# A new order of scores, values and outputs at the 64 attention slices of a gated cross-attention and feed-forward block

## Chip, cores and metric

One Trainium2 chip, one core. The metric is the device time of one execution in microseconds (us). Engines: PE is TensorE (matmuls; PEld its weight loads), DVE is VectorE, ACT is ScalarE, POOL is GpSimd, SP the queue that issues the DMAs.

## The reference, cut to what matters

```python
# x, ctx: (32, 64, 512); 8 key heads, 4 query heads for each, head size 128; causal inside each 64 rows
x = x + tanh(g_xattn) * attention(layernorm(x), ctx, ctx, Wq, Wk, Wv) @ Wd.T
x = x + tanh(g_ffn) * ffn(layernorm(x))
# attention: scores = Q K^T / sqrt(128), masked, softmax over the keys, times V
# ffn: down(silu(gate(x)) * up(x)), each weight being w * (su @ sv), inner size 1792
```

All is float32. Every large product is made as three products of fp32r numbers (high*high, high*low, low*high), so each operand is first split into `hi` (ACT copies it to fp32r) and `lo` (DVE or POOL subtracts).

## The kernel before

The 2048 rows are 16 tiles of 128. The program is written engine by engine, in an order set by hand, with semaphores between the engines; nothing reorders it. Stages: keys of half the chunks, then 56 "quads" `quad(q)` (values, keys, queries; also the effective ffn weights through `effective`), then 64 units of attention, then 28 steps of the ffn. A unit `u` is one key head and one chunk of 256 rows, two units are a pair, `NU = 64`, `NPAIR = 32`. The last three quads already hold the first units: `scores(0)`, `scores(1)` stand before quad 53 (`NQ - 3`), `scores(2)`, `scores(3)` before quad 55, `weighted_values(0)` inside it.

What one unit takes, with the lines of the profile:
- `scores(u)`, L697: 8 matmuls of K (128 rows, 64 columns of weights) by Q into one PSUM bank, `score_bank(u)`, 6 for even and 7 for odd units.
- `turned` (DVE transpose out of the bank, L1334), `masked` (POOL, L1657), `maxima` (DVE, L1338), `other_maxima` (four small ACT copies, L1022), `row_maxima` (DVE, L1344), `less_max` (POOL, L1663), `exponentials` (ACT, L1035), `sums` (DVE, L1348), `other_sums` (four ACT copies, L1030), `inverse` (DVE, L1352 and L1356), `over_sum` (POOL, L1669), `probs_turned` (DVE, L1362). Maxima and sums are shared by the two units of a pair.
- `weighted_values(u)`, L722: 8 matmuls with 64-row weights, into two banks; `out_hi` (ACT, two halves, L1042) and `out_lo` (DVE, two halves, L1375) split the result.
- `output(i)`, `i = 2u` and `2u + 1`: 12 matmuls of 512 columns (L574) into one bank; `add_to_x(i)` (DVE, L1386) adds it to the rows `X`. `output_hi`, `output_lo` (ACT L1015, POOL L1649) split the four heads of the next output weights; each takes 1 of 4 `e`.

PE's loop body of pair p (u = 2p), before: scores(u), scores(u+1), output(2u-7), output(2u-6), weighted_values(u-2), weighted_values(u-1), output(2u-5), output(2u-4).

In pairs 18, 21, 24, 27 (`ROWS1`) the second layernorm of two finished tiles is started: `stats2`, `ln_moments` (DVE, L1239 to L1250), `ln_pow` (POOL, L1600), `apply2` (POOL, L1677, two passes). One pair later (`COLUMNS1`) `columns2` transposes them on PE (L751) into banks 2 and 3 between output(2u-7) and output(2u-6), `x2_columns` (ACT, L1050, L1053) empties these banks, and `x2_sums` (POOL) combines; weighted_values(u-1), which writes the same banks, waits for `x2_columns`. Another pair later (`SPLIT1`) come `x2_hi_of` (ACT, L1068) and `x2_lo_of` (DVE, L1410).

Two waits matter later and are the same in both kernels: `out_hi(u-1)` overwrites what output(2u-5) reads, and so waits for that output's end; `out_lo` of it follows.

Of the kernel before, what the change touches and what calls it, by code (L numbers as in the profile page):

```python
# [21 lines left out]
NU = HKV * NCH  # L22
# [29 lines left out]
def flamingo(nc, es, x, ctx_t, g_xattn, g_ffn, w1, wq, wd, wf, sf_l, sf_r, out):  # L52
# [150 lines left out]
    a_c0, a_chi, a_k, a_w1, a_tanh = sem("a_c0"), sem("a_chi"), sem("a_k"), sem("a_w1"), sem("a_tanh")  # L203
    a_xt, a_xhi, a_wa, a_s1, a_s5, a_c11 = (sem("a_xt"), sem("a_xhi"), sem("a_wa"), sem("a_s1"), sem("a_s5"),
# [87 lines left out]
    def output_bank(i):  # L292
        if i >= 2 * NU - 4:
            return 4 + i - (2 * NU - 4)
        return 6 if i % 4 == 3 else (3 * (i // 4) + i % 4) % 2

    def output_before(i):

        n = 3 * (i // 4) + i % 4 - 2
        return 4 * (n // 3) + n % 3  # L300

    def score_bank(u):
        return 6 + u % 2
# [34 lines left out]
    def _(sp):  # L338
# [148 lines left out]
        for q in range(NQ):  # L487
            quad_dmas(q)
            if q == NQ - 3:
                load_wd(1)  # L490
            if q == NQ - 2:
                load_q_k(2)
                load_q_k(3)
            if q == NQ - 1:
# [5 lines left out]
                load_v(3)  # L500
            if q == Q0 + NHP:
# [67 lines left out]
    def _(pe):  # L569
# [42 lines left out]
        def effective(m):  # L612
# [4 lines left out]
            if m == E_AT[NQ - 3]:  # L617
                pe.wait_ge(v_turn, 2)
            if m == E_AT[NQ - 1]:
                pe.wait_ge(v_turn, 4)  # L620
# [63 lines left out]
        def scores(u):  # L684
# [41 lines left out]
        def output(i):  # L726
# [20 lines left out]
        def columns2(m, banks):  # L747
            for p in range(2):
                pe.wait_ge(g_xn, 2 * m + p + 1)
# [14 lines left out]
        output(0)  # L764
        for p in range(2, NPAIR):
            u = 2 * p
            scores(u)
            scores(u + 1)
            output(2 * u - 7)
# [5 lines left out]
            weighted_values(u - 1)  # L775
# [1081 lines left out]
```

## Time and profile before

| | us |
|---|---|
| median of 3 runs (1431.50, 1431.82, 1435.93) | 1431.82 |
| the profiled execution | 1430.72 |
| its span | 1428.7 |
| outside the span | 2.0 |
| PE busy / DVE busy / POOL busy / ACT busy | 1400.6 / 1016.2 / 1038.6 / 640.3 |

A profile row gives start and duration, the engine, the source line and the operation, and in square brackets the idle time of the engine just before it with what ended it. Matmuls overlap in a pipeline: a row of one is longer than the distance to the next. The granted TensorE clock is 1.00 in all stretches but a few us.

### The profile page before, as it was taken

To read this page: it belongs to the slowest core of one execution; us is meant where nothing else is said; L and a number is where in the kernel's file an instruction comes from. 1 tells how busy PE (TensorE), PEld (TensorE's weight loads), DVE (VectorE), ACT (ScalarE), POOL (GpSimd) and SP (SyncE) were. 2 spreads that over 40 slices of the span, in tenths; PEclk is the share of its full clock that TensorE was granted. 3 is DMA by queue.
4 is the path that set the end of the run, shared out by engine and by line. 5 is a ranking of instruction groups with operands and counts; after the bars stand their busy time and mean duration, and the time that the engine had idled before them with its cause. 6 is when DMAs were issued, how large, how long until landed. Compare 5 with 4: busy or idle time off the path is not lost.

```text
span 1428.7 us, 19944 instructions
## 1 busy us (share of the span) xinstructions
PE 1400.6 (98%) x6810; PEld 1125.3 (79%) x6810; DVE 1016.2 (71%) x1549; ACT 640.3 (45%) x1246; POOL 1038.6 (73%) x919
## 2 busy tenths in 40 slices
PE   8999999999999999999999999999999999999998
PEld 8988788888887767777776766767888888888887
DVE  6487777777465677777776776775688878676776
ACT  6465555554444344443443444444344434343433
POOL 5599999998879556656656777775678886666664
PEclk9999999999999999999999999999999999999999
DMA  8477787778887745434443433331112112212112
GB/s 282 150 251 226 233 270 257 253 254 282 307 264 264 254 156 199 140 125 142 135 152 118 155 116 120 127 132 31 45 45 60 52 45 65 105 47 65 45 59 74
DMA packets 116067, 217.96 MB, mean 153 GB/s; under 512 B 9472, under 2 KB 47616, under 8 KB 113920
## 3 DMA queue, kind: packets, MB, share of 16 engines
q1 hardware_dynamic: 115968, 216.70, 46.1%
q8 instruction: 55, 0.90, 0.3%
q14 instruction: 44, 0.36, 0.1%
HBM read 151.13 MB, written 65.54 MB: 152 GB/s over the span
## 4 chain that ended last, share of the span: by engine, by line
PE 82%; POOL 8%; DVE 4%; issue 3%; ACT 1%; DMA 1%; SPq 0%; DVEq 0%; POOLq 0%; ACTq 0%
PE bank L574 65%; PE bank L848 3%; PE bank L849 3%; PE bank L850 3%; PE bank L697 3%; PE bank L722 3%; POOL prob L1663 2%; POOL xn L1677 1%; POOL wd_lo L1649 1%; POOL prob L1657 1%; POOL prob L1669 1%; DVE X L1386 1%; POOL wa_lo L1643 1%; PE bank L621 1%; DMA q_sb<-q_scratch 0%
## 5 line engine op out<-in xcount | busy, mean ns | idle before, releaser
L574 PE MATMUL bank<-xc,wa_hi 128*128 128x512 f32 x896 | 277.4, 391 | 0.0
L574 PE MATMUL bank<-wd_hi,o_hi 128*128 128x512 f32 x512 | 207.9, 406 | 5.0 <-issue 3.5
L574 PE MATMUL bank<-wd_lo,o_hi 128*128 128x512 f32 x512 | 200.8, 392 | 0.0
L574 PE MATMUL bank<-wd_hi,o_lo 128*128 128x512 f32 x512 | 199.5, 390 | 0.0
L574 PEld LDWEIGHTS bank<-xc,wa_hi 128*128 128x128 f32 x896 | 167.7, 188 | 36.4 <-issue 1.1
L574 PE MATMUL bank<-xc,wa_lo 128*128 128x512 f32 x448 | 174.5, 390 | 0.0
L1455 DVE SCALAR_TENSOR_TENSOR X<-bank,tg,X 128x512 f32<-128x512 f32 x221 | 154.5, 742 | 0.0
L574 PE MATMUL bank<-x_hi,wf_hi 128*128 128x512 f32 x392 | 153.0, 390 | 0.0
L574 PE MATMUL bank<-x_hi,wf_lo 128*128 128x512 f32 x392 | 152.6, 389 | 0.0
L574 PE MATMUL bank<-x_lo,wf_hi 128*128 128x512 f32 x364 | 141.7, 389 | 0.0
L1669 POOL TENSOR_TENSOR prob<-prob,row_inv 128x512 f32<-128x512 f32 x64 | 72.5, 1153 | 94.6 <-DVE row_inv L1356 94.6
L1386 DVE SCALAR_TENSOR_TENSOR X<-bank,tg,X 128x512 f32<-128x512 f32 x128 | 94.7, 741 | 65.2 <-PE bank L574 65.2
L574 PEld LDWEIGHTS bank<-wd_hi,o_hi 128*128 128x128 f32 x512 | 96.1, 188 | 47.9 <-issue 27.7
L574 PEld LDWEIGHTS bank<-wd_hi,o_lo 128*128 128x128 f32 x512 | 96.3, 188 | 21.3
L574 PEld LDWEIGHTS bank<-wd_lo,o_hi 128*128 128x128 f32 x512 | 96.3, 188 | 17.7
L1022 ACT ACTIVATE other_max<-own_max 32x32 f32<-32x32 f32 x128 | 29.1, 227 | 178.8 <-DVE own_max L1338 176.4
L1657 POOL TENSOR_TENSOR prob<-prob,mask 128x512 f32<-128x512 f32 x64 | 81.2, 1290 | 34.5 <-DVE prob L1334 34.5
L1300 DVE TENSOR_TENSOR t<-bank,s 128x512 f32<-128x512 f32 x44 | 30.3, 689 | 99.9 <-PE bank L574 99.7
L1375 DVE TENSOR_TENSOR o_lo<-bank,o_hi 128x512 fp32r<-128x512 f32 x128 | 82.1, 684 | 23.4 <-ACT o_hi L1042 23.4
L574 PEld LDWEIGHTS bank<-xc,wa_lo 128*128 128x128 f32 x448 | 84.1, 188 | 17.9
L1643 POOL TENSOR_TENSOR wa_lo<-w_raw,wa_hi 128x512 fp32r<-128x512 f32 x72 | 76.5, 1084 | 24.8 <-ACT wa_hi L951 24.7
L1643 POOL TENSOR_TENSOR wa_lo<-ws,wa_hi 128x1024 fp32r<-128x1024 f32 x36 | 92.5, 2570 | 0.0
(181 smaller groups left out, 3424.7 us busy)
## 6 DMA issues: line engine op xcount, KB each, us to landing
q_scratch<-q_st SPq DMA_DIRECT2D x32, 1024.0 KB, 4.4
q_sb<-q_scratch SPq DMA_DIRECT2D x64, 512.0 KB, 4.9
w_raw<-in_wq SPq DMA_DIRECT2D x32, 512.0 KB, 4.4
wd_raw<-in_wd SPq DMA_DIRECT2D x16, 1024.0 KB, 5.1
f_raw<-ffn_eff_scratch SPq DMA_DIRECT2D x28, 512.0 KB, 3.6
er_raw<-in_sf_r SPq DMA_DIRECT2D x42, 256.0 KB, 3.9
e_raw<-in_wf SPq DMA_DIRECT2D x42, 256.0 KB, 5.4
ffn_eff_scratch<-e_eff SPq DMA_DIRECT2D x42, 256.0 KB, 5.2
```

The lines of the kernel that those rows point to most:

```text
L574: last = pe.matmul(to, a, b, start=(start and n == 0), stop=(stop and n == 3 * len(pairs) - 1), skip_group_check=onto)
L697: last = pe.matmul(bank[score_bank(u)][b * S:(b + 1) * S, t * 256:(t + 1) * 256], k_sb[u % 2][:, cb * S:(cb + 1) * S], q_sb[u % 2][:, :, c ...
L722: last = pe.matmul(bank[value_bank(u) + b][:, t * 256:(t + 1) * 256], v_sb[u % 2][rows, t, :], pt_of(u)[rows, t, :], start=True, stop=True)
L848: pe.matmul(to, d_hi[b][:, half, cols], dn_hi[n == NF - 1][:, :], start=True, stop=False)
L849: pe.matmul(to, d_hi[b][:, half, cols], dn_lo[n == NF - 1][:, :], start=False, stop=False)
L850: pe.matmul(to, d_lo[b][:, half, cols], dn_hi[n == NF - 1][:, :], start=False, stop=True).then_inc(p_yf, 1)
L1375: v.tensor_tensor(lo, bank[value_bank(u) + b][:, :].rearrange("p (t e s) -> p t e s", t=CT, e=G), f32(hi), ALU.subtract).then_inc(v_o, 1)
L1386: v.scalar_tensor_tensor(to, bank[output_bank(i)][:, :], tg[:, 0:1], to, ALU.mult, ALU.add).then_inc(v_y, 1)
L1455: v.scalar_tensor_tensor(to, bank[down_bank(n, k)][:, :], tg[:, 1:2], to, ALU.mult, ALU.add).then_inc(v_yf, 1)
L1643: g.tensor_tensor(wa_lo[p][:, part, :, :].rearrange("p n k d -> p (n k d)"), raw, f32(wa_hi[p][:, part, :, :]).rearrange("p n k d -> p (n ...
L1657: g.tensor_tensor(to, to, mask[:, :].rearrange("p (o k) -> p o k", o=1).broadcast_to([P, NR // 2, S]), ALU.add).then_inc(g_mask, 1)
L1669: g.tensor_tensor(to, to, row_inv[:, u % 2, :].rearrange("p (n o) -> p n o", o=1).broadcast_to([P, NR, HS]), ALU.mult).then_inc(g_p, 1)
```

## The change

The entry and the loop over the pairs get a new order on all engines. On PE the loop body becomes output(2u-7), output(2u-6), weighted_values(u-2), weighted_values(u-1), scores(u+2), scores(u+3), output(2u-5), output(2u-4): the scores stand directly behind the values and are made one pair earlier. Score banks change: units 1 and 3 use bank 5; in the loop, bank 6 is shared with the outputs i % 4 == 1 (before: 3). The engines' lists are moved to suit; `apply2` goes from POOL to ACT, with a shift made on POOL; of each four output-weight heads three are split in even pairs and one in odd pairs; loads of queries and keys are issued earlier.

```diff
@@ banks
-        return 6 if i % 4 == 3 else (3 * (i // 4) + i % 4) % 2
+        return 6 if i > 1 and i % 4 == 1 or i == 2 * NU - 5 else (3 * (i // 4) + SHARED[i % 4]) % 2 if i > 1 else i
+    SHARED = (0, None, 1, 2)
     def score_bank(u):
-        return 6 + u % 2
+        return 5 if u in (1, 3) else 6 + u % 2
     def value_bank(u):
-        return 6 if u == NU - 1 else 2 if u % 2 else 4
-    WD_STEP = {2 * k + 2 + n: (k + 1, (2 * n, 2 * n + 1)) for k in range(NWD - 1) for n in range(2)}
+        return 6 if u in (1, NU - 1) else 2 if u % 2 else 4
+    WD_STEP = {2 * k + 2 + n: (k + 1, ((0, 1, 2), (3,))[n]) for k in range(NWD - 1) for n in range(2)}
@@ SP
         for q in range(NQ):
+            if q == NQ - 2:
+                load_q_k(2)
+                load_q_k(3)
             quad_dmas(q)
...
-            if q == NQ - 2:
-                load_q_k(2)
-                load_q_k(3)
...
+                load_q_k(6)
+                load_q_k(7)
...
-            for n in range(u + 2, min(u + 4, NU)):
-                load_q_k(n)
             load_v(u)
             load_v(u + 1)
+            for n in range(u + 4, min(u + 6, NU)):
+                load_q_k(n)
@@ PE, effective: two waits on v_turn removed; scores
-            if u in (1, 3, 5):
-                pe.wait_ge(v_e, E_AT[(NQ - 4, NQ - 2, NQ - 1)[u // 2]] + 1)
-            if u >= 6 and u % 2 == 0:
-                pe.wait_ge(v_y, 2 * u - 8)
+            if u >= 8 and u % 2 == 0:
+                pe.wait_ge(v_y, 2 * u - 10)
+            if u == 1:
+                pe.wait_ge(a_xt, 16)
+            if u in (4, 5):
+                pe.wait_ge(v_o, 4)
@@ PE, weighted_values
             if u == 0:
-                pe.wait_ge(a_xt, 16)
+                pe.wait_ge(v_turn, 4)
             elif u == 1:
+                pe.wait_ge(v_turn, 3)
+                pe.wait_ge(v_e, NP)
+            elif u == 3:
                 pe.wait_ge(v_c12, NQ)
                 pe.wait_ge(v_c21, NQ)
@@ PE, output
-            elif i < 2 * NU - 4 and i % 4 == 3:
-                pe.wait_ge(v_turn, min(2 * ((i + 5) // 4), NU - 2) + 1)
+            elif i == 2 * NU - 5:
+                pe.wait_ge(v_y, i - 1)
+            elif i == 2:
+                pe.wait_ge(v_y, 2)
+            elif i < 2 * NU - 4 and i % 4 == 1:
+                pe.wait_ge(v_turn, min((i + 7) // 2, NU - 2) + 1)
@@ PE, the loop
         weighted_values(1)
         output(0)
+        output(1)
+        scores(4)
+        scores(5)
         for p in range(2, NPAIR):
             u = 2 * p
-            scores(u)
-            scores(u + 1)
-            output(2 * u - 7)
+            if p > 2:
+                output(2 * u - 7)
             if p in COLUMNS1:
                 pe.wait_ge(v_o, 2 * u - 4)
                 columns2(COLUMNS1[p], (2, 3))
             output(2 * u - 6)
             weighted_values(u - 2)
             weighted_values(u - 1)
+            if p + 1 < NPAIR:
+                scores(u + 2)
+                scores(u + 3)
             output(2 * u - 5)
             output(2 * u - 4)
@@ ACT
+            if q == NQ - 1:
+                other_maxima(1)
...
+        def apply2(m):
+            a.wait_ge(g_nm, 8 + m + 1)
+            if m:
+                a.wait_ge(p_xt2, 2 * m)
+            for p in range(2):
+                a.activation(xn2[:, p, :], X[:, 2 * m + p, :], ACT.Identity, bias=shift[:, p:p + 1],
+                             scale=rstd[:, p:p + 1]).then_inc(a_xn2, 1)
...
         for p in range(2, NPAIR):
             u = 2 * p
+            exponentials(u)
+            exponentials(u + 1)
+            other_sums(p)
             if p in WD_STEP:
                 k, heads = WD_STEP[p]
                 for e in heads:
                     output_hi(k, e)
             if p in COLUMNS1:
                 x2_columns(COLUMNS1[p], (2, 3))
-            other_maxima(p)
             out_hi(u - 2)
-            exponentials(u)
-            exponentials(u + 1)
+            out_hi(u - 1)
+            if p in ROWS1:
+                apply2(ROWS1[p])
             if p in SPLIT1:
                 x2_hi_of(SPLIT1[p])
-            other_sums(p)
+            if p + 1 < NPAIR:
+                other_maxima(p + 1)
...
-            out_hi(u - 1)
@@ DVE, the last quad: maxima(2), maxima(3), row_maxima(1), out_lo(0) moved in; then
+        out_lo(1)
         sums(2)
         sums(3)
+        add_to_x(0)
         inverse(1)
+        turned(4)
+        turned(5)
+        probs_turned(2)
+        probs_turned(3)
+        add_to_x(1)
+        maxima(4)
+        maxima(5)
+        row_maxima(2)
         for p in range(2, NPAIR):
             u = 2 * p
+            if p > 2:
+                add_to_x(2 * u - 8)
             sums(u)
             sums(u + 1)
+            if p > 2:
+                add_to_x(2 * u - 7)
             inverse(p)
             if p in ROWS1:
                 stats2(ROWS1[p])
                 ln_moments(8 + ROWS1[p])
+            add_to_x(2 * u - 6)
+            out_lo(u - 2)
+            if p + 1 < NPAIR:
+                turned(u + 2)
+                turned(u + 3)
+            probs_turned(u)
+            probs_turned(u + 1)
+            out_lo(u - 1)
+            add_to_x(2 * u - 5)
+            if p in SPLIT1:
+                x2_lo_of(SPLIT1[p])
+            if p + 1 < NPAIR:
+                maxima(u + 2)
+                maxima(u + 3)
+                row_maxima(p + 1)
@@ POOL
         for p in range(2, NPAIR):
             u = 2 * p
-            over_sum(u - 2)
-            over_sum(u - 1)
-            masked(u)
-            masked(u + 1)
+            over_sum(u)
+            over_sum(u + 1)
             if p in COLUMNS1:
                 x2_sums(COLUMNS1[p])
+            if p in ROWS1:
+                ln_pow(8 + ROWS1[p])
             if p in WD_STEP:
                 k, heads = WD_STEP[p]
+                output_lo(k, heads[0])
+            if p + 1 < NPAIR:
+                masked(u + 2)
+                masked(u + 3)
...
+                for e in heads[1:]:
                     output_lo(k, e)
-            less_max(u)
-            less_max(u + 1)
-            if p in ROWS1:
-                ln_pow(8 + ROWS1[p])
-                apply2(ROWS1[p])
+            if p + 1 < NPAIR:
+                less_max(u + 2)
+                less_max(u + 3)
```

## Rows read from the trace of the kernel before

**Rows 1.** The page's first section: PE's busy time.
```profile
PE 1400.6 (98%) x6810; PEld 1125.3 (79%) x6810; DVE 1016.2 (71%) x1549; ACT 640.3 (45%) x1246; POOL 1038.6 (73%) x919
```
**Rows 2.** Stretches: us, busy of PE, PEld, DVE, ACT, POOL (instructions), clock, DMA share, GB/s.
```profile
529.63:757.23 227.60, 227.60 (x1203) 170.66 (x1202) 163.64 (x285) 96.21 (x241) 137.40 (x121) 1.00 0.46 151
757.23:943.15 185.92, 173.65 (x915) 129.41 (x914) 133.64 (x232) 80.05 (x188) 135.11 (x117) 0.99 0.38 125
```
**Rows 3.** Chain that ended last: one pair (start us, us, what).
```profile
590.33 1.93 PE bank L722 x16
592.25 5.71 PE bank L574 x24
597.96 1.88 PE bank L697 x16
599.84 5.66 PE bank L574 x24
```
**Rows 4.** The same view in a quad: 24 matmuls in a row without a change of kind.
```profile
303.82 5.46 PE bank L574 x24
```
**Rows 5.** Timeline, third period: when ACT, DVE take up the values and outputs.
```profile
591.44 1.09 ACT L1042 ACTIVATE o_hi<-bank 128x512 fp32r<-128x512 f32 x2 [0.84 <-PE bank L722]
...
592.14 1.29 DVE L1375 TENSOR_TENSOR o_lo<-bank,o_hi 128x512 fp32r<-128x512 f32 x2 [0.92 <-ACT o_hi L1042]
...
602.82 0.75 DVE L1386 SCALAR_TENSOR_TENSOR X<-bank,tg,X 128x512 f32<-128x512 f32 x1 [0.47 <-PE bank L574]
```
**Rows 6.** Timeline, 501 to 510 us: the softmax chain of units 2 and 3, undisturbed.
```profile
501.94 1.27 DVE L1338 TENSOR_REDUCE own_max<-prob 128x16 f32<-128x512 f32 x2
...
504.26 0.19 DVE L1344 TENSOR_TENSOR row_max<-own_max,other_max 128x32 f32<-128x32 f32 x1 [1.05 <-ACT other_max L1022]
...
504.53 2.06 POOL L1663 TENSOR_TENSOR prob<-prob,row_max 128x512 f32<-128x512 f32 x2 [7.67 <-DVE row_max L1344]
...
507.28 0.69 DVE L1348 TENSOR_REDUCE own_sum<-prob 128x16 f32<-128x512 f32 x1 [0.32 <-ACT prob L1035]
...
508.00 0.98 ACT L1030 ACTIVATE other_sum<-own_sum 32x32 f32<-32x32 f32 x4 [0.75 <-DVE own_sum L1348]
...
509.24 0.35 DVE L1356 RECIPROCAL row_inv<-row_sum 128x32 f32<-128x32 f32 x1
...
509.67 2.05 POOL L1669 TENSOR_TENSOR prob<-prob,row_inv 128x512 f32<-128x512 f32 x2 [3.09 <-DVE row_inv L1356]
```
**Rows 7.** Timeline of pairs 18 to 20, and PE in pair 23 (834 us).
```profile
763.34 1.22 DVE L1239 BATCH_NORM_STATS2 bn<-X 128x6 f32<-128x512 f32 x2
...
763.79 1.15 ACT L1015 ACTIVATE wd_hi<-wd_raw 128x512 fp32r<-128x512 f32 x2
...
765.93 4.14 POOL L1677 TENSOR_SCALAR xn<-X,moments,rstd 128x512 f32<-128x512 f32 x2
...
770.70 0.60 ACT L1053 ACTIVATE xb<-bank 128x512 f32<-128x512 f32 x1
...
782.65 0.69 DVE L1348 TENSOR_REDUCE own_sum<-prob 128x16 f32<-128x512 f32 x1 [0.32 <-ACT prob L1035]
...
784.14 1.95 PE L697 MATMUL bank<-q_sb,k_sb 128*64 128x256 f32 x16 [0.99 <-DVE X L1386]
...
795.37 1.69 ACT L1068 ACTIVATE x_hi<-xb 128x1792 fp32r<-128x1792 f32 x1
...
798.59 1.96 DVE L1410 TENSOR_TENSOR x_lo<-xb,x_hi 128x1792 fp32r<-128x1792 f32 x1
...
834.08 3.07 PE L697 MATMUL bank<-q_sb,k_sb 128*64 128x256 f32 x16 [2.75 <-DVE X L1386]
```
**Rows 8.** What PE waited for: line, releaser: us in total, times, longest.
```profile
PE bank L722 <- DVE q_st L1318: 1.8, 1, 1.8
...
PE bank L697 <- DVE e_eff L1272: 0.8, 1, 0.8
...
PE bank L697 <- DMA q_sb<-q_scratch: 0.5, 1, 0.5
```

More of the change, by code:

```diff
@@ L616, in effective @@
                 pe.wait_ge(v_e, m)
[L617 to L620, printed above, removed]
             pe.matmul(bank[7][:, :], el[:96, :], er[:96, :], start=True, stop=True).then_inc(p_e, 1)
@@ L748, in columns2 @@
             for p in range(2):
-                pe.wait_ge(g_xn, 2 * m + p + 1)
+                if m < 4:
+                    pe.wait_ge(a_xn2, 2 * m + p + 1)
+                else:
+                    pe.wait_ge(g_xn, 2 * (m - 4) + p + 1)
                 for k in range(KC):
@@ L1180, in _ @@
         out_hi(0)
-        other_maxima(1)
         exponentials(2)
         exponentials(3)
+        out_hi(1)
         other_sums(1)
-        out_hi(1)
+        other_maxima(2)
         for p in range(2, NPAIR):
             u = 2 * p
+            exponentials(u)
+            exponentials(u + 1)
+            other_sums(p)
             if p in WD_STEP:
@@ L1242, in ln_moments @@
             v.wait_ge(v_bn, 2 * n + 2)
-            if 1 <= n <= 8:
+            if 1 <= n <= 12:
                 v.wait_ge(g_nm, n)
@@ L1294, in quad @@
                 inverse(0)
+                maxima(2)
                 probs_turned(0)
+                maxima(3)
                 probs_turned(1)
+                row_maxima(1)
             v.wait_ge(p_p[7], q + 1)
@@ L1302, in quad @@
                 effective(E_AT[q])
+            if q == NQ - 1:
+                v.wait_ge(a_tanh, 1)
+                out_lo(0)
             v.wait_ge(v_t2, q + 1)
@@ L1390, in stats2 @@
             if m:
-                v.wait_ge(g_xn, 2 * m)
+                if m <= 4:
+                    v.wait_ge(a_xn2, 2 * m)
+                else:
+                    v.wait_ge(g_xn, 2 * (m - 4))
             ln_bn(lambda p: X[:, 2 * m + p, :])
@@ L1479, in _ @@
             quad(q)
-        v.wait_ge(a_tanh, 1)
-        out_lo(0)
-        maxima(2)
-        maxima(3)
-        row_maxima(1)
+        out_lo(1)
         sums(2)
         sums(3)
+        add_to_x(0)
         inverse(1)
+        turned(4)
[6 more added lines that the diff above has]
+        row_maxima(2)
         for p in range(2, NPAIR):
             u = 2 * p
-            add_to_x(2 * u - 8)
-            out_lo(u - 3)
-            turned(u)
-            turned(u + 1)
-            probs_turned(u - 2)
-            probs_turned(u - 1)
-            add_to_x(2 * u - 7)
-            maxima(u)
-            maxima(u + 1)
-            add_to_x(2 * u - 6)
-            row_maxima(p)
-            out_lo(u - 2)
+            if p > 2:
+                add_to_x(2 * u - 8)
             sums(u)
             sums(u + 1)
-            add_to_x(2 * u - 5)
+            if p > 2:
+                add_to_x(2 * u - 7)
             inverse(p)
-            if p in SPLIT1:
-                x2_lo_of(SPLIT1[p])
             if p in ROWS1:
@@ L1510, in _ @@
                 ln_moments(8 + ROWS1[p])
+            add_to_x(2 * u - 6)
[13 more added lines that the diff above has]
+                row_maxima(p + 1)
         add_to_x(2 * NU - 8)
-        out_lo(NU - 3)
-        probs_turned(NU - 2)
-        probs_turned(NU - 1)
         for i in range(2 * NU - 7, 2 * NU - 4):
@@ L1599, in ln_pow @@
                 g.wait_ge(a_xn, 2 * n)
+            elif 8 < n <= 12:
+                g.wait_ge(a_xn2, 2 * (n - 8))
             g.tensor_tensor(rstd[:, :], veps[:, :], neg_half[:, :], ALU.pow).then_inc(g_pow, 1)
-            if n < 8:
+            if n < 12:
                 g.wait_ge(g_pow, n + 1)
@@ L1757, in _ @@
             if q == NQ - 1:
+                masked(2)
+                masked(3)
                 over_sum(0)
                 over_sum(1)
-                masked(2)
-                masked(3)
             if q + 2 < NCH:
@@ L1787, in _ @@
         less_max(3)
+        over_sum(2)
+        over_sum(3)
+        masked(4)
+        masked(5)
+        less_max(4)
+        less_max(5)
         for p in range(2, NPAIR):
             u = 2 * p
-            over_sum(u - 2)
-            over_sum(u - 1)
-            masked(u)
-            masked(u + 1)
+            over_sum(u)
+            over_sum(u + 1)
             if p in COLUMNS1:
                 x2_sums(COLUMNS1[p])
+            if p in ROWS1:
+                ln_pow(8 + ROWS1[p])
             if p in WD_STEP:
                 k, heads = WD_STEP[p]
-                for e in heads:
-                    output_lo(k, e)
-            less_max(u)
-            less_max(u + 1)
-            if p in ROWS1:
-                ln_pow(8 + ROWS1[p])
-                apply2(ROWS1[p])
+                output_lo(k, heads[0])
+            if p + 1 < NPAIR:
+                masked(u + 2)
+                masked(u + 3)
+            if p in WD_STEP:
+                for e in heads[1:]:
+                    output_lo(k, e)
+            if p + 1 < NPAIR:
+                less_max(u + 2)
+                less_max(u + 3)
             if p == F_FIRST:
@@ L1808, in _ @@
                     ffn_left_lo(0, part)
-        over_sum(NU - 2)
-        over_sum(NU - 1)
         for n in range(NF):
```

7 lines of the change are left out of this document (4 added, 3 removed).

## The prediction

> **What bounds the kernel now.** I read the page's busy times first: PE is busy 1400.6 of 1428.7 us [rows 1], so a reorder can win only the idle 28 us and what PE's busy time contains beside plain streaming. Next the stretches [rows 2]. Fifteen pairs of the attention loop take 227.60 us, 15.17 each, with no idle PE at all; the next eleven take 185.92, with 12.27 idle (185.92 less 173.65). At 15.17 they would take 166.9, so 19.0 us hang on the four layernorm groups there. Then the chain through one pair [rows 3]: values 1.93, 24 output matmuls 5.71, scores 1.88, 24 outputs 5.66. In a quad 24 such matmuls without a change of kind take 5.46 [rows 4], 0.2275 each. So PE loses 0.20 behind scores and 0.25 behind values although it never looks idle. Last the waits [rows 8], which show the holes at the entry.
>
> **Part 1: one change of kind less per pair.** Before, a pair has four: to scores, to outputs, to values, to outputs. After, values and scores adjoin and 48 output matmuls run in one piece. If values still take 1.93 up to the next kind and scores 1.88 [rows 3], the period is 1.93 + 1.88 + 0.20 + 48 x 0.2275 = 14.93, against 15.17: 0.245 less. It holds for pairs 3 to 30, 28 of them: 6.9 us. Values directly followed by scores do not occur in the trace. Bounds: such a change costs nothing (another 0.2 per pair gained) or twice (nothing gained). I take one ordinary change, since all four seen cost alike, 0.20 to 0.25. By the Trainium skill (TensorEngine Tiling, Key Properties) "Changing tiling mode (not just tile) drains the TensorE"; values use 64-row and scores 64-column weights, so by that page this border drains too, and the gain is no more than one change; a free border would give some 6 us more. No run here shows that border.
>
> **Part 2: does the new period hold?** Time zero is the start of weighted_values(u-2). Scores start at 1.93, output(2u-5) at 3.81, and its end is noticed 2.98 later (602.82 less 599.84, [rows 3, 5]), at 6.79. The wait on this output holds out_hi(u-1); out_lo follows 0.70 behind it (592.14 less 591.44, [rows 5]) at 7.49 and holds DVE 1.2, add_to_x(2u-5) 0.67 (rows of 1.29 and 0.75 less their overlap, [rows 5]), so maxima start at 9.36. From there, as in [rows 6]: row_max 2.32 later, less_max 0.27, the second sums 2.75: 14.70. The next scores(u+4) go to bank 6 and wait for add_to_x(2u-3), which is queued on DVE behind these sums: 1.49 from the sums to the scores (784.14 less 782.65, [rows 7]), so 16.19. PE wants it at 14.93 + 1.93 = 16.86. The slack is 0.67 us: thin, but no stall. The masks end by 8.3 even in an even pair, the two further weight heads by 10.9, less_max wants POOL at 11.95. Everything else is early: the probabilities of the values are turned at about 6.5 and read at 14.93, loads have over 8 us for about 5. With the old order the same chain had the scores as its start, now their result is needed a pair later; it is the shared bank 6 that ties them.
>
> **Part 3: the layernorm groups.** Gone from POOL is apply2, 4.14 us [rows 7], which stood before over_sum and was what made PE wait 0.99 and 2.75 at the scores. ACT does it in two passes, at 7.9 to about 9.5 in the first pair; nothing waits there, other_maxima comes at 10.7 or later. But three other places now cost:
> - Pair 18, 21, 24, 27: the statistics stand on DVE ahead of turned; 1.22 [rows 7] and 0.5 for the small ones take the DVE's 1.0 us of spare time before out_lo(u-1) and push maxima 0.58. Slack covers it.
> - The pair behind (19, 22, 25, 28): x2_columns stands on ACT behind exponentials, other_sums and the weight heads. The second sums start at 14.70 + 0.58 - 14.93 - 0.8 (the transposes, which hold PE but not this chain: an estimate, most of the 1.3 worked out below) = -0.5. other_sums end 0.72 + 0.98 later [rows 6], 1.2. One head (odd pair) or three (even) at 0.575 (1.15 for two, [rows 7]) and two copies of 0.60 plus gaps, 1.27 [rows 7], end at 3.05 or 4.2. weighted_values(u-1) wants these banks at 0.97 and waits: 2.2 or 3.35 us, with scores and outputs queued behind it on PE, whose operands are ready. Before, ACT was free and did the copies at once.
> - The pair behind that (20, 23, 26, 29): x_hi follows out_hi(u-1), 7.9 to 9.6 (1.69, [rows 7]), x_lo 9.7 to 11.6 (1.96, [rows 7]) stands ahead of maxima, which start 2.2 late; less 0.67 slack, scores(u+4) wait 1.55.
> Of the 19.0 before, 12.3 are idle and 1.6 one fall of the clock (rival E); the other 5.1, 1.3 per group, are transposes and restarts, and stay. After: 1.3 + 1.55 + 2.2 or 3.35, 5.05 or 6.2 per group, 22.5 in all, against 17.4 without the clock's part; I keep one fall on both sides. The groups lose 5.1 us: the long POOL pass is gone, but the waits that come in its place are longer.
>
> **Part 4: the entry.** The wait of scores(1) for e_eff, 0.8, goes (bank 5), and so does that of scores(3) for its DMA, 0.5 [rows 8], as the loads move ahead of a quad's; with 0.3 for the late scores(2) the last quad starts 1.85 earlier. weighted_values(1) no longer waits 1.8 for q_st [rows 8]. Then comes output(0), output(1), scores(4), scores(5), and output(2) waits for add_to_x(1), which is on DVE behind turned(5) and both probs_turned: 0.65 + 1.25 + 0.74 and latencies, 2.9 us. output(4) waits for out_lo(2), behind three weight heads on ACT: 1.2. The values of pair 3 then start at about 527.9 (529.63 before, [rows 2]), and the next scores wait 0.9. Net 0.8 gained.
>
> **The sum.** Against the profiled execution, 1430.72: -6.9 - 0.8 + 5.1 = -2.6, 1428.1. The median of the runs lies 1.1 above that execution, so I forecast 1429.2 for the median. The ffn and the quads are untouched; the last pairs have no wait and get none.
>
> **Rivals.**
> - A, the border is free: 29 x 0.2 more, 1423. For: the scores' weights are the smaller ones. Against: all borders cost alike.
> - B, the border costs double, so that the order doesn't do what it says: 6.9 given back, 1436.
> - C, slower: the chain through bank 6 is longer than I have it. It decides from 0.67 us on; each further 0.1 costs 2.8 us over 28 pairs. At 1.0 (0.33 over) it costs 9 and the kernel ends at 1438.4. For: the pieces are taken from different moments, and POOL's neighbours change. Against: each piece is a measured distance.
> - D, the values' wait for x2_columns is far shorter (the copies are reached before the heads, or the chain is ahead): up to 11 us less, 1418.
> - E, the clock. The wait of 2.75 was followed by half clock: scores 3.07 instead of 1.95 [rows 7] and slower outputs, 1.6 us; the window's mean is 0.99 [rows 2]. A wait of the same length in pair 29 was not. New waits of 2.9 and 3.35 twice could each do it: three more falls, 4.8, give 1434. The Trainium skill (TensorE: Matmul & The Clock Gate) says too that activity releases the throttle; by it more falls are likelier the longer the waits, which is this case.
>
> **Chances.** Forecast 0.45 (of it 0.15 below 1427.5), A 0.12, B 0.07, C 0.15, D 0.12, E 0.09. A measurement tells about 0.3%, 4.3 us, from no change. Faster: 0.15 + 0.12 + 0.12 = 0.39. Slower (over 1436.1): C and half of B, 0.18. Same: 0.43. The forecast alone is 1425 to 1433; faster and slower cases both count, so the range goes from 1419 (A whole, most of D left out) to 1438.4 (C at its price).
>
> **What will show it.** In the steady pairs: period 14.93, 48 outputs in 11.1 without a gap, scores directly behind values in 1.9; the DVE row of add_to_x(2u-3) ending 0.5 to 0.8 before scores; a gap in front of scores in each pair means C. In the groups: a gap inside the values of 2 to 3.5 us with ACT xb (L1050) as its cause, and one of 1.5 at scores behind X (L1386); POOL without 4.14. At the entry 2.9 at output(2). I am wrong if a group's gaps are below 2 us in sum, or the period differs from 14.93 by over 0.1.

## The result, and the profile after

| | before | after |
|---|---|---|
| median, us | 1431.66 (4 runs, 1430.30 to 1435.93) | 1443.30 (4 runs, 1443.01 to 1444.92) |
| ratio after / before | | 1.0079, interval 1.0056 to 1.0101 |
| profiled execution | 1430.72 | 1443.34 |
| its span | 1428.7 | 1441.6 |

The change is slower by 11.6 us. The forecast was 1429.2 with a range from 1419 to 1438.4. The page first:

```profile
PE 1402.2 (97%) x6810; PEld 1131.6 (78%) x6810; DVE 993.8 (69%) x1553; ACT 641.1 (44%) x1254; POOL 1024.4 (71%) x915
```

As against [rows 1], PE is busy 1.6 us more and idle 11.3 us more (1441.6 - 1402.2 = 39.4, before 28.1). One pair of the steady part in the chain that ended last (start us, us, what), to be set beside [rows 3]:

```profile
590.09 1.93 PE bank L728 x16
592.02 1.88 PE bank L700 x16
593.89 11.11 PE bank L579 x48
```

The values (L728) now border on the scores (L700) and cost 1.93 before the scores begin, exactly what they cost before outputs begin. The period is 605.00 - 590.09 = 14.91. So the gain is there; what PE waited for shows where it went (line, releaser: us in total, times, longest):

```profile
PE bank L728 <- ACT xb L1080: 11.5, 4, 3.2
PE bank L579 <- DVE o_lo L1411: 6.9, 3, 5.8
PE bank L700 <- DVE X L1422: 6.0, 4, 1.5
...
PE bank L579 <- DVE X L1422: 2.7, 1, 2.7
```

The first line is the values' wait for x2_columns (four times), the third the scores' wait for add_to_x behind x_lo (four times), the last the wait of output(2) at the entry: all three forecast. The second was not: 5.8 us in one piece, and two of 0.6. Stretches of the changed kernel (us, busy of PE, PEld, DVE, ACT, POOL, clock, DMA, GB/s): 15 steady pairs counted from the values of unit 4 (it begins and ends within 0.9 us of that), the eleven pairs with the layernorm groups, the last two pairs, and three short pieces around a wait and what follows it.

```profile
530.41:754.98 224.57, 224.57 (x1209) 172.76 (x1210) 163.54 (x288) 94.42 (x242) 136.18 (x119) 1.00 0.46 153
754.13:946.44 192.31, 175.06 (x915) 131.67 (x914) 134.21 (x237) 83.97 (x196) 120.45 (x113) 0.96 0.36 121
961.28:1004.13 42.85, 35.58 (x171) 27.82 (x170) 21.17 (x36) 13.93 (x32) 24.95 (x25) 0.92 0.10 32
509.00:516.00 7.00, 5.08 (x18) 3.92 (x20) 3.84 (x7) 2.17 (x6) 3.90 (x4) 0.76 0.47 164
822.00:834.00 12.00, 8.78 (x42) 5.43 (x42) 6.23 (x11) 4.52 (x11) 8.53 (x9) 0.72 0.28 86
981.00:993.00 12.00, 6.23 (x20) 4.71 (x19) 7.45 (x13) 4.85 (x12) 7.69 (x8) 0.72 0.23 75
```

With the starts of the values (V) of some units as marks, in both profiled executions:

| stretch | before | after | difference | forecast |
|---|---|---|---|---|
| start to the first scores | 462.3 | 464.6 | +2.3 | 0 |
| first scores to V(4) | 67.3 | 65.8 | -1.5 | -1.7 |
| V(4) to V(34), 15 pairs | 227.6 | 223.7 | -3.9 | -3.7 and 0.9 of wait |
| V(34) to V(56), 11 pairs | 185.9 | 192.3 | +6.4 | +0.9 |
| V(56) to V(60) | 30.4 | 31.4 | +1.0 | +1.0 |
| V(60) to V(62) | 18.5 | 26.3 | +7.8 | 0 |
| V(62) to the end | 436.7 | 437.5 | +0.8 | 0 |
| sum | | | +12.9 | -2.6 |

(The forecast's column is the prediction's sum cut at these marks; the last of its four waits of 1.55 falls behind V(56).)

### The profile page after: what moved, and what is told of

Same layout as the page of the kernel before. It is cut to its first block, busy times and chain, and to the rows that moved or that the text cites. A ratio compares the mean times of both kernels' runs of the same rounds, so it can differ in the third digit from the quotient of the medians.

```text
span 1441.6 us, 19962 instructions
## 1 busy us (share of the span) xinstructions
PE 1402.2 (97%) x6810; PEld 1131.6 (78%) x6810; DVE 993.8 (69%) x1553; ACT 641.1 (44%) x1254; POOL 1024.4 (71%) x915
## 4 chain that ended last, share of the span: by engine, by line
PE 71%; POOL 16%; DVE 5%; issue 4%; ACT 4%; DMA 1%; DVEq 0%; POOLq 0%; ACTq 0%
PE bank L579 54%; POOL wa_lo L1690 6%; PE bank L700 4%; PE bank L728 4%; PE bank L865 3%; PE bank L866 3%; PE bank L867 3%; POOL ws L1678 1%; POOL prob L1710 1%; POOL ws L1681 1%; POOL ws L1679 1%; POOL wf_lo L1757 1%; POOL ws L1683 1%; DVE own_max L1374 1%; DVE o_lo L1411 1%
## 5 line engine op out<-in xcount | busy, mean ns | idle before, releaser
L1716 POOL TENSOR_TENSOR prob<-prob,row_inv 128x512 f32<-128x512 f32 x64 | 65.9, 1050 | 97.3 <-DVE row_inv L1392 97.3
L1710 POOL TENSOR_TENSOR prob<-prob,row_max 128x512 f32<-128x512 f32 x64 | 66.0, 1052 | 85.8 <-DVE row_max L1380 85.8
L1061 ACT ACTIVATE o_hi<-bank 128x512 fp32r<-128x512 f32 x128 | 68.8, 591 | 104.6 <-PE bank L579 101.9
L1333 DVE TENSOR_TENSOR t<-bank,s 128x512 f32<-128x512 f32 x44 | 30.4, 691 | 106.2 <-PE bank L579 106.2
L1690 POOL TENSOR_TENSOR wa_lo<-ws,wa_hi 128x1024 fp32r<-128x1024 f32 x36 | 100.9, 2804 | 0.0
L1757 POOL TENSOR_TENSOR wf_lo<-f_raw,wf_hi 128x512 fp32r<-128x512 f32 (+1 forms) x56 | 57.5, 1028 | 55.4 <-ACT wf_hi L1103 55.2
```

What stands on the lines that cost most here:

```text
L1061: a.activation(o_hi[u % 2][:, :, :].rearrange("p e (t b s) -> p b t e s", t=CT, b=2)[:, b], bank[value_bank(u) + b][:, :].rearrange("p (t ...
L1690: g.tensor_tensor(wa_lo[p][:, part, :, :].rearrange("p n k d -> p (n k d)"), raw, f32(wa_hi[p][:, part, :, :]).rearrange("p n k d -> p (n ...
L1710: g.tensor_tensor(to, to, row_max[:, u % 2, :].rearrange("p (n o) -> p n o", o=1).broadcast_to([P, NR, HS]), ALU.subtract).then_inc(g_sub, 1)
L1716: g.tensor_tensor(to, to, row_inv[:, u % 2, :].rearrange("p (n o) -> p n o", o=1).broadcast_to([P, NR, HS]), ALU.mult).then_inc(g_p, 1)
L1757: g.tensor_tensor(wf_lo[:, cols, :, :].rearrange("p n k d -> p (n k d)"), raw, f32(wf_hi[:, cols, :, :]).rearrange("p n k d -> p (n k d)") ...
```

## The experiments

All kernels but the two of the old order start from the changed one. What was to be told apart: my theory is that every microsecond of the loss is a queue order, an instruction ahead of another on ACT, DVE or POOL that PE then waits for, and half clock behind such a wait. Rivals: the chip gives the loss elsewhere (the first 460 us), or the new order has so little slack that each cured wait comes back as another.

A fall of the clock is here a stretch with a granted clock of 0.50 instead of 1.00 (1.2 instead of 2.4 GHz).

### The end: the ffn split in pair 31

```diff
@@ ACT, loop
             out_hi(u - 2)
+            if p == F_FIRST + 1:
+                for part in range(3):
+                    gate_up_hi(0, part)
             out_hi(u - 1)
...
-            if p == F_FIRST:
-                for part in range(3):
-                    gate_up_hi(0, part)
@@ POOL, loop
             if p == F_FIRST:
                 ffn_left_sums(0)
+            if p == F_FIRST + 1:
                 for part in range(3):
                     ffn_left_lo(0, part)
```

> The changed kernel, with one thing moved: the first step's ffn weights are split on ACT (and their low parts on POOL) in pair 31 instead of pair 30, so that ACT does not stand at them in front of the exponentials of units 62 and 63. Theory (the late loss is this queue order): the wait of 5.8 us before output(120) shrinks to under 1, the half clock of 6.8 us behind it goes, in all 8 to 9 us less than the changed kernel, about 1434.5. Rival (DVE or the weight heads hold that output anyway): the wait stays at 4 or more and the time within 3 us of 1443.

Measured: 1439.06 us (1438.84 to 1439.58), 4.2 less. In the changed kernel ACT, POOL and PE stood like this (timeline, 975 to 989 us):

```profile
975.56 0.40 ACT L1108 ACTIVATE wf_hi<-f_raw 128x256 fp32r<-128x256 f32 x1
...
979.50 0.73 POOL L1751 TENSOR_TENSOR fs<-f_raw,fs 128x256 f32<-128x256 f32 x1
...
980.27 1.06 ACT L1114 ACTIVATE wf_hi<-fs 128x1024 fp32r<-128x1024 f32 x1 [4.31 <-POOL fs L1751]
981.23 1.14 ACT L1054 ACTIVATE prob<-prob 128x512 f32<-128x512 f32 x2
...
988.52 0.77 PE L579 MATMUL bank<-wd_hi,o_hi 128*128 128x512 f32 x1 [5.77 <-DVE o_lo L1411]
```

ACT waits 4.31 us at the third part of gate_up_hi for POOL's sums (`ffn_left_sums`), which stand behind less_max; the exponentials of units 62 and 63, whose input is complete at 977.4, are queued behind it, and behind them sums, other_sums, the weight head, out_hi(60), out_lo(60) and output(120). In the old order gate_up_hi stood behind the exponentials that take up the less_max of the same pair (units 60 and 61), and those of 62 and 63 came a pair later; in the new order gate_up_hi lies between less_max and its exponentials. With the move the wait is 1.5 us, for out_hi, and V(60) to V(62) falls from 26.3 to 20.3. These 6.0 us are less than the 8 to 9 of the theory, which had left no wait over 1 us; the half clock behind the wait did go. Of the 6.0 some 1.8 are missing in the total: the first scores stood 0.8 us later in this execution, and V(34) to V(56) took 1.2 us more. There two of the waits of the scores were 2.65 us instead of 1.50 (a fall at 933 us came, and the long one at 825 was half as long). The cause of the longer waits is one that neither theory nor rival had. `x2_lo_of` on DVE and a weight head on POOL run at the same time there, and one of them is stretched. First the changed kernel, then this one (POOL and DVE, at the first such place of each):

```profile
797.46 4.40 POOL L1696 TENSOR_TENSOR wd_lo<-wd_raw,wd_hi 128x512 fp32r<-128x512 f32 x2
798.69 2.03 DVE L1449 TENSOR_TENSOR x_lo<-xb,x_hi 128x1792 fp32r<-128x1792 f32 x1
...
796.86 2.55 POOL L1696 TENSOR_TENSOR wd_lo<-wd_raw,wd_hi 128x512 fp32r<-128x512 f32 x2
798.11 3.18 DVE L1449 TENSOR_TENSOR x_lo<-xb,x_hi 128x1792 fp32r<-128x1792 f32 x1
```

Where POOL gave way (4.40 instead of 2.55), x_lo took 2.03 and the next scores waited 1.50; where DVE gave way, x_lo took 3.18 and they waited 2.65.

### The groups: x2_columns first

```diff
@@ ACT, loop
+            if p in COLUMNS1:
+                x2_columns(COLUMNS1[p], (2, 3))
             exponentials(u)
             exponentials(u + 1)
             other_sums(p)
...
-            if p in COLUMNS1:
-                x2_columns(COLUMNS1[p], (2, 3))
             out_hi(u - 2)
```

> The changed kernel, with x2_columns first in ACT's pair, ahead of exponentials. Theory: the four waits inside the values (2.5, 3.2, 2.6, 3.1 us, 11.5 in sum) go to nothing, and with them most of the half clock in 770 to 950 us (13.6 us at half, some 6 us lost): 15 to 17 us less, about 1427. Rival (the exponentials pushed back by 1.3 us make the scores' wait on bank 6 longer by as much): only 6 to 10 us less, with waits at scores of 2.5 us or more. Second rival (the half clock has another cause than these waits): 11.5 us less, the half clock still there.

Measured: 1432.55 us (10 runs, 1430.02 to 1434.62), ratio to the kernel before 0.9997 (0.9988 to 1.0007). That is 10.8 us less than the changed kernel, between the theory and the rival. The waits inside the values are gone (the cause is shown), and in 754 to 950 us only one fall of the clock is left. But the odd pairs have a new wait of 2.1 and 2.2 us. PE and POOL there (timelines):

```profile
772.58 0.74 POOL L1730 TENSOR_TENSOR xb<-xb 128x256 f32<-128x256 f32 x1
...
775.47 1.27 POOL L1696 TENSOR_TENSOR wd_lo<-wd_raw,wd_hi 128x512 fp32r<-128x512 f32 x1
...
776.95 0.47 PE L579 MATMUL bank<-wd_hi,o_hi 128*128 128x512 f32 x1 [2.09 <-DVE o_lo L1411]
```

The profile names o_lo, but PE starts 0.21 us after the end of wd_lo (776.74): the fourth head of the output weights, which in the new split of heads is made in the odd pair, stands on POOL behind the four x2_sums. The values' wait had covered it. Neither theory nor rival had this one.

### Three moves

The two above, and at the entry:

```diff
@@ DVE, entry
         inverse(1)
+        add_to_x(1)
         turned(4)
         turned(5)
         probs_turned(2)
         probs_turned(3)
-        add_to_x(1)
```

> The changed kernel with three moves: the split of the ffn weights in pair 31, x2_columns ahead of the exponentials, and add_to_x(1) ahead of turned(4) at the entry. Theory: the waits add up, 8 to 9 + 15 to 17 + 4.4 (2.7 wait and 1.7 of half clock at the entry), so 27 to 30 us less than the changed kernel, about 1415, and so about 17 below the kernel before. Rival (the loss lies elsewhere, in the quads or in the order as such): above 1425.

Measured: 1426.13 us (1425.38 to 1427.27), ratio 0.9954 (0.9939 to 0.9969): 17.2 less than the changed kernel, where 27 to 30 were expected. 1426.13 also lies just above the 1425 from which the rival on record (the loss lies elsewhere) was to hold; the next experiment answers that. The entry gave nothing: output(2) no longer waits, but output(4) does, 2.9 us, for out_hi(2), which stands on ACT behind exponentials, other_sums and three weight heads; half clock followed as before. First scores to V(4) take 67.1 us, against 65.8. So at that place the first wait had hidden the second.

### The output weights ahead of the sums, x_lo behind row_maxima

The end and x2_columns as above, not the entry, and

```diff
@@ POOL, loop
-            if p in COLUMNS1:
-                x2_sums(COLUMNS1[p])
...
                 less_max(u + 2)
                 less_max(u + 3)
+            if p in COLUMNS1:
+                x2_sums(COLUMNS1[p])
@@ DVE, loop
-            if p in SPLIT1:
-                x2_lo_of(SPLIT1[p])
             if p + 1 < NPAIR:
                 maxima(u + 2)
                 maxima(u + 3)
                 row_maxima(p + 1)
+            if p in SPLIT1:
+                x2_lo_of(SPLIT1[p])
```

> The changed kernel with the ffn split in pair 31, x2_columns ahead of the exponentials, and two more moves in the layernorm groups: x2_sums at the end of POOL's pair (behind less_max) and x2_lo_of behind row_maxima on DVE. Theory (the 2.1 us before output in the odd pairs is the fourth weight head, queued on POOL behind x2_sums; the 1.5 at scores is x_lo ahead of maxima): both kinds go, the stretch from the values of unit 34 to those of unit 56 falls from 179.7 us (the kernel with three moves) to about 171, the kernel ends at 1418 to 1420. Rival (x_lo behind row_maxima runs beside less_max and holds POOL's reads, so the scores wait as long or longer): the 1.5 us waits stay, the stretch stays over 176 and the time over 1423.

Measured: 1415.81 us (1415.08 to 1417.50), ratio 0.9882 (0.9862 to 0.9902). The stretch V(34) to V(56):

```profile
754.32:926.98 172.66, 167.98 (x914) 129.01 (x913) 133.89 (x237) 84.40 (x196) 119.75 (x111) 1.00 0.41 135
```

172.7 us, 7 less than with three moves (179.7) and 19.6 less than the changed kernel. The wait behind x2_sums is gone, so its cause is shown. The wait of the scores only went from 1.5 to 1.1, and here the rival on record had the mechanism right, though not its size. x_lo now runs beside less_max, and POOL is held:

```profile
796.80 2.02 DVE L1449 TENSOR_TENSOR x_lo<-xb,x_hi 128x1792 fp32r<-128x1792 f32 x1
796.96 3.77 POOL L1710 TENSOR_TENSOR prob<-prob,row_max 128x512 f32<-128x512 f32 x2 [1.13 <-DVE row_max L1380]
```

less_max takes 3.77 us in all four groups and 2.06 in the other pairs. 1.71 more, less the slack of 0.67, is 1.04 of the 1.12 measured.

### One part of the change alone, in the old order

The kernel before, with apply2 on ACT behind the weight heads of the next pair:

```diff
@@ ACT, loop of the kernel before (apply2 as in the change)
             if p in COLUMNS1:
+                apply2(COLUMNS1[p])
                 x2_columns(COLUMNS1[p], (2, 3))
             other_maxima(p)
@@ POOL
                 ln_pow(8 + ROWS1[p])
-                apply2(ROWS1[p])
```

> The kernel before with one part of the change alone: the two layernorm passes of apply2 go from POOL to ACT (with the shift on POOL), all orders kept, ACT takes them behind the weight heads of the next pair. Theory (the 4.14 us on POOL ahead of over_sum were the whole cause of the four holes of 2.75 us): the holes go or fall under 0.5, the one stretch of half clock too, 10 to 13 us less than the kernel before, about 1420. Rival (the statistics on DVE and the combining on POOL hold the chain as well): 4 to 7 us less.

Measured: 1417.78 us (1416.10 to 1418.97), ratio 0.9898 (0.9881 to 0.9914): 15.2 us less than the kernel before measured beside it (1433.02). Its two stretches, to be set beside [rows 2]:

```profile
529.89:757.49 227.60, 227.60 (x1201) 170.65 (x1201) 163.64 (x285) 96.15 (x241) 137.48 (x121) 1.00 0.46 151
757.49:927.92 170.43, 170.31 (x914) 128.62 (x913) 132.91 (x236) 85.75 (x196) 119.70 (x113) 1.00 0.42 136
```

The first is unchanged, the second is 15.5 us shorter with 0.1 us idle. The POOL passes of 4.14 [rows 7] were the whole cause of the holes, as the theory said, and the gain is even above its 10 to 13: 170.4 is 11 x 15.17 = 166.9 and 3.5 for four sets of transposes, so that of my 1.3 us "transposes and restarts" per group only 0.9 are transposes.

### The border between kinds

The kernel with three moves, with output(2u-5) between the values and the scores:

```diff
@@ PE, loop
             weighted_values(u - 1)
+            output(2 * u - 5)
             if p + 1 < NPAIR:
                 scores(u + 2)
                 scores(u + 3)
-            output(2 * u - 5)
             output(2 * u - 4)
```

> The kernel with three moves, but output(2u-5) put between the values and the scores, so that a pair has four changes of kind on PE again (values, outputs, scores, outputs), all else of the new order kept. Theory (the gain of the new order is one change of kind per pair): steady period back at 15.17 from 14.92 us. Rival (the gain comes from somewhere else, as banks or the longer distance of the chain): the period stays under 15.0.

Measured once: fifteen pairs take

```profile
530.53:758.13 227.60, 227.60 (x1201) 170.67 (x1201) 162.90 (x285) 93.07 (x238) 136.36 (x119) 1.00 0.45 151
```

15.17 each, the old period to the hundredth, with PE never idle. One pair of it (chain, start us, us, what):

```profile
636.81 1.93 PE bank L728 x16
638.74 2.98 PE bank L579 x12
641.73 1.88 PE bank L700 x16
643.61 8.38 PE bank L579 x36
```

The first twelve outputs, behind the values, take 0.25 more than 12 x 0.2275, the 36 behind the scores 0.19 more than 36 x 0.2275. So the 0.26 us per pair come with the fourth change of kind. (The whole kernel takes 1439.87 us, with new waits of 2.2 to 2.8 in the groups and of 3.2 at the entry; only its period counts here.)

### All moves at once, and the old order with bank 5

To the moves above comes out_hi(u-2) ahead of the weight heads; x_hi and x_lo go ahead of out_hi(u-1) and out_lo(u-1); and at the entry out_hi(2) goes ahead of the exponentials and out_lo(2) ahead of the sums:

```diff
@@ ACT, loop
+            if p == 2:
+                out_hi(2)
             exponentials(u)
             exponentials(u + 1)
             other_sums(p)
+            if p > 2:
+                out_hi(u - 2)
...
                     output_hi(k, e)
+            if p in SPLIT1:
+                x2_hi_of(SPLIT1[p])
@@ DVE, loop
+            if p == 2:
+                add_to_x(2)
+                out_lo(2)
             sums(u)
             sums(u + 1)
...
             probs_turned(u + 1)
+            if p in SPLIT1:
+                x2_lo_of(SPLIT1[p])
             out_lo(u - 1)
```

> All moves at once: ffn split in pair 31, x2_columns first, x2_sums at POOL's end, out_hi(u-2) ahead of the weight heads, x_hi and x_lo ahead of out_hi(u-1) and out_lo(u-1), and at the entry add_to_x(1) ahead of turned(4), out_hi(2) ahead of the exponentials, out_lo(2) ahead of the sums. Theory (all waits of the changed kernel are queue orders, the new period of 14.92 us is sound): stretch of unit 34 to 56 about 169 us, entry without a wait over 1 us, 1409 to 1412, some 6 below the old order with the layernorm passes on ACT. Rival (the new order has too little slack and turns each cured wait into another): 1417 or more, no better than that old order.

Measured: 1414.21 us (1411.90 to 1414.46), ratio 0.9869 (0.9851 to 0.9887), between the 1409 to 1412 of the theory and the 1417 of the rival; V(34) to V(56) 171.7 us (expected 169). At the entry, where no wait over 1 us was expected, scores(8) wait 2.8 us and half clock follows.

The same entry with out_lo(2) in DVE's own wait for other_sums:

```diff
@@ DVE, loop
-            if p == 2:
-                add_to_x(2)
-                out_lo(2)
             sums(u)
             sums(u + 1)
+            if p == 2:
+                out_lo(2)
...
             inverse(p)
```

> The kernel with all moves, with out_lo(2) at the entry between the sums and their inverse, in the time in which DVE waits for other_sums, rather than ahead of the sums. Theory (the 2.8 us wait of scores(8), with half clock behind it, is the chain of the pair pushed back by add_to_x(2) and out_lo(2)): it falls to 1 us or less and the half clock goes, 2 to 4 us less than the kernel with all moves, 1410 to 1412. Rival (output(4) now waits instead, for out_lo(2)): 1414.

Measured: 1412.61 us (1412.28 to 1413.64), ratio 0.9861 (0.9846 to 0.9875), just above the 1410 to 1412 expected. The wait of scores(8) is 1.7 us, not under 1, with a new one of 0.95 before an output; no half clock in the loop.

The old order, with apply2 on ACT and one more part of the change (with it go PE's waits of the first scores and values and of `effective`, which are set much as in the change):

```diff
@@ on the old order with apply2 on ACT
     def score_bank(u):
-        return 6 + u % 2
+        return 5 if u in (1, 3) else 6 + u % 2
@@ SP
         for q in range(NQ):
+            if q == NQ - 2:
+                load_q_k(2)
+                load_q_k(3)
             quad_dmas(q)
```

> The old order with the layernorm passes on ACT, and with one more part of the change: scores 1 and 3 in bank 5, and the loads of units 2 and 3 ahead of quad 54's DMAs. Theory: the waits of 0.8, 0.4 and 0.5 us before the scores go, the later ones of 1.8 and 1.4 stay: the values of unit 4 come 1.7 us earlier after the first scores, 1416. Rival (PE gets there earlier but the queries' sums on DVE hold the second values longer): nothing gained, 1417.8.

> The old order with the layernorm passes on ACT, bank 5 and the earlier loads, once more, beside the best kernel of the new order: 1414 as before. If the new order is worth its 0.25 us per pair with all waits cured, the other kernel of this call is 2 to 4 us below it; if its small remaining waits (4 x 0.75 and 0.6 us in the layernorm groups, 1.1 at the end) eat the gain, they are level within 1 us.

Measured: 1414.07 us (1413.94 to 1414.53), ratio 0.9872 (0.9855 to 0.9889), and measured again 1414.46 (1413.69 to 1414.89), ratio 0.9871 (0.9855 to 0.9888). The first scores to V(4) take 65.1 us (67.3 without the part; 1.7 were expected to go, and 1416 in all). Measured beside the second of these, the best kernel of the new order (the one just above) is 1.9 us lower; the runs of the two do not overlap, the intervals of their ratios do. The new order with its waits mostly cured is worth about that, of 7 us that 28 shorter periods make. Its two stretches, against those of the old order with apply2 on ACT:

```profile
525.89:751.38 225.49, 223.77 (x1202) 172.05 (x1201) 161.88 (x288) 96.82 (x241) 137.20 (x121) 1.00 0.45 152
751.38:922.98 171.60, 168.03 (x914) 129.02 (x913) 134.31 (x237) 85.71 (x196) 119.88 (x111) 1.00 0.41 135
```

In the groups it is 1.2 us longer than the old order (170.4) although each pair is 0.25 shorter: 3.6 us of waits are left.

### The changed kernel again

> The changed kernel once more, unaltered. Up to the first scores its instructions are those of the kernel before, yet its first scores stood at 464.6 us and those of five other kernels with the same beginning between 462.3 and 465.4. Theory (the phase of DVE and POOL in the quads falls out by chance in each execution): the first scores lie somewhere in that span, more than 0.3 us from 464.6, and the waits of the attention loop are the same to 0.1 us. Rival (the place is fixed by the kernel's code): within 0.3 us of 464.6.

Measured: 1446.48 us. The first scores stand at 464.65 us, within 0.1 of the first execution: by what was expected the rival (the place is fixed by the code) holds. The waits are the same (2.73, 2.49, 3.19, 2.66, 3.20, 5.72), but for one of the scores, at 914 us: it is 2.67 us instead of 1.50 (x_lo takes 3.21 us there instead of 2.02, beside the weight head), and one more fall of the clock follows at 934. These two make most of the 3.1 us by which the span is longer than in the first execution. Not all is fixed by the code, though: the old order with bank 5, run twice, had its first scores at 462.70 and 463.42.

## Why the prediction was wrong, point by point

- **Part 1, the border.** Right. The period is 14.91 (forecast 14.93), and the values next to the scores cost what they cost next to outputs (1.93), which also settles rivals A and B. The kernel with the border put back has 15.17.
- **Part 2, slack of 0.67.** Right: no wait in any steady pair, so rival C fell. That the slack is about this size shows in the groups, where the maxima start 2.2 us late behind x_lo (11.6 us after the values instead of 9.4) and the scores wait 1.5.
- **Part 3, the groups.** The waits were right within 0.4 us one by one: forecast 2.2 and 3.35 inside the values (its own terms, 3.05 and 4.2 less 0.97, make 2.1 and 3.2), measured 2.49, 3.22, 2.60, 3.14; forecast 1.55 at the scores, measured 1.50 three times (1.50 the fourth, in V(56) to V(60)). What was mis-sized is the clock behind them, rival E. I kept one fall; there were falls behind three of the four waits in the values, one of them long. The chain's rows behind them:

```profile
773.35 1.72 PE bank L728 x8
775.07 2.93 PE bank L700 x16
...
826.37 2.08 PE bank L728 x8
828.45 3.54 PE bank L700 x16
...
879.31 1.86 PE bank L728 x8
881.16 2.79 PE bank L700 x16
...
932.32 1.13 PE bank L728 x8
933.46 1.88 PE bank L700 x16
```

  The last two rows are the same work at full clock behind an equally long wait. The first six cost 0.6 + 1.05, 0.95 + 1.66, 0.7 + 0.9 more: 5.9 us. That, less the one fall of 1.6 that the forecast kept, is 4.3 of the 5.5 us by which this stretch missed. Most of the other 1.2 are the two waits of 0.60 and 0.57 us of an output for o_lo, which the prediction did not have. I had given E a chance of 0.09 and held its price as three more falls; there were five places with one in the whole of this execution and six in the next. The rows of before already showed one fall for two waits of 2.75, and I forecast three waits of that size or more (2.9, and 3.35 twice) and put no fall for them into the sum. That is the first step that failed.
- **Part 4, the entry.** Output(2) was to wait 2.9, measured 2.73. The waits of output(4) (forecast 1.2) and of scores(8) (0.9) did not show in this execution, because half clock (0.76 in 509 to 516 us) took their place. Two kernels with the same entry whose clock did not fall there show it: with x2_columns first, and with the sums behind the output weights, output(4) waits 0.72 and scores(8) 0.54, and from V(0) to V(34) all three take the same 258.8 to 258.9 us. So the fall cost nothing at this place, and the 1.7 us for it among the 4.4 expected of the move at the entry were not there to be won. With three moves the wait of output(4) appeared with 2.9. Two sums of this part don't come out of their terms: 0.8, 0.5 and 0.3 make 1.6 and not 1.85 (measured: the values of unit 0 start 30.6 us behind the first scores, before 32.7), and the 1.7 us by which V(4) comes earlier can't be had from the terms that are named; the wait of 1.4 for o_lo, which went too, is missing among them. That 1.5 was measured is in part luck.
- **The sum: "the last pairs have no wait and get none."** This sentence was the second step that failed, and the dearest: it put at nothing what measured 7.8 us. Without it the kernel would have ended at 1435.5, inside the range. I had worked out a general pair and the three kinds of layernorm pairs on all engines, and not pair 30, where gate_up_hi and ffn_left_sums stand in the same queues. The diff leaves these lines as they are; but what directly follows less_max on ACT, the exponentials, stood in front of them and now stands behind them. What is not in a diff's changed lines can still change its place.
- **The quads.** "The ffn and the quads are untouched": 2.3 us of loss up to the first scores, in which the instructions are the same. In the thirteen profiled executions of this study the first scores lie between 462.3 and 465.4. The prediction put it at nothing. What sets it stays open: the repeat speaks for the code of the kernel, the twice-run old order against it.
- **Rival D** fell: the values waited in full.
- **The tail.** 0.8 us more from V(62) to the end. They lie behind PE's last matmul, and the eleven other executions have them too (437.4 to 437.5), those of the old order with apply2 on ACT among them; only the one of the kernel before has 436.7. So they are no sign against the new order; their cause stays open.

Together: 7.8 (end) + 5.5 (the groups: 4.3 of clock, 1.2 of waits) + 2.3 (quads) + 0.8 (the tail) less 0.9 (the wait of pair 3 that did not come; what is left at the entry and in the steady pairs cancels) make the 15.5 us between -2.6 and +12.9. The direction of the loss is settled by the runs: with the end, x2_columns, x2_sums and x_lo moved, the same order is 16 us below the kernel before. And one part of the change, apply2 on ACT, gives 15.2 of it in the old order; in the new one it does not show, as other waits had taken the place of POOL's.

## What to carry to other kernels

When a reorder makes a period shorter by a fraction of a microsecond, walk every pair that has something extra in a queue, to the last one, and list for each added piece what now stands behind it; unchanged lines count. A wait on PE of 2 us or more has to be priced with the half clock that may follow: here about 1.6 us for a fall, 2.6 for a long one, and next to nothing where PE would soon have waited anyway. Try the parts of a change singly: here the one that mattered (a pass off the POOL queue) was hidden by the order that came with it, and a cured wait often uncovers the next, as the fourth weight head behind x2_sums. And before a pass is moved to a free stretch of its own engine, look at what the neighbouring engine does there: x_lo took 2.0 us alone, but beside POOL's work it or that work took 1.2 to 1.9 us more.

## What the runs showed of the hardware

- A change between 128x128 weights, 64-row weights and 64-column weights costs PE 0.19 to 0.26 us in these periods (14.91 us with three changes, 15.17 with four), and it is not counted as idle time of PE (227.60 busy of 227.60). By the Trainium skill (TensorEngine Tiling, Key Properties) a change of the tiling mode drains the engine; the trace agrees in so far as each change costs time, and no row shows the drain itself.
- Waits of 2.1 us already were followed by half clock in some places (2.09 at 777 us with x2_columns first) and not in others (2.09 at 778 us with three moves, and 3.14 at 929 us in the changed kernel, where the repeat had it). In the changed kernel a fall stood at five of the six waits from 2.49 us up. Over the thirteen profiled executions, from 50 us on, PE waited 2.09 us or longer 37 times, and the clock fell during 26 of these waits or within 1.5 us of their end; of 108 waits of 0.4 to 1.8 us none had one, and but for the last microseconds of each execution there was no other fall.
- A DVE subtraction with two SBUF inputs (x_lo, 128x1792) and POOL instructions that run at the same time hold each other up, now one and now the other: x_lo 3.18 to 3.21 us instead of 2.03 with the weight head unchanged, or one head of 3.14 instead of 1.3 with x_lo unchanged, and less_max 3.77 instead of 2.06. The stretched x_lo and the stretched head were seen three times each, at the same places of the loop (in both executions of the changed kernel and with the ffn split moved), and the scores' wait behind them differs by 1.2 us, between two executions of one kernel too.
- POOL's tensor_scalar with two per-partition operands takes 2.08 us for 128x512, the same function as one ACT pass 0.8:

```profile
761.96 1.52 ACT L1070 ACTIVATE xn<-X,shift,rstd 128x512 f32<-128x512 f32 x2
```

  against 4.14 for two on POOL [rows 7].
